# A scheduled attention loop: VectorE's scores issued every three tiles in a free row group, its value products and the transposes moved, the key tail in four small products

## The reference, cut to what matters

```python
def _L0_xattn_ref(query, key_value, Wq, bq, Wk, bk, Wv, bv, Wo, bo):
    ...
    q = (query @ Wq + bq).reshape(B, Nq, H, D).transpose(0, 2, 1, 3)
    k = (key_value @ Wk + bk).reshape(B, Nkv, H, D).transpose(0, 2, 1, 3)
    v = (key_value @ Wv + bv).reshape(B, Nkv, H, D).transpose(0, 2, 1, 3)
    attn = jnp.einsum('bhqd,bhkd->bhqk', q, k) * scale
    attn = jnp.clip(attn, -CLAMP, CLAMP)
    attn = jax.nn.softmax(attn, axis=-1)
    ...
    x = jnp.einsum('bhqk,bhkd->bqhd', attn, v).reshape(B, Nq, Cq)
    return x @ Wo + bo

x = x + _L0_xattn_ref(_layernorm(x, axis=-1), ctx_768, ...)
x = x + _L0_ffn_ref(_layernorm(x, axis=-1), ...)
```

## Time and profile before

| what | us |
|---|---|
| median of 3 runs | 830.57 |
| lowest, highest | 828.7, 833.89 |
| the profiled execution's own time | 830.38 |
| its span (first to last instruction) | 828.6 |
| TensorE busy with products | 748.6 |
| ScalarE busy | 726.7 |
| VectorE busy | 553.2 |
| exps of the loop (L497), 500 | 680.2 |

### The profile page before, as it was taken

The page is one execution under the profiler, slowest core; times in us unless marked ns, Lnnn a source line. Parts: engine busy times, 40 slices in busy tenths (PEclk is TensorE's granted clock), DMA queues, the critical chain, the costliest instruction groups (busy, mean ns, idle before and its releaser), DMA issues.

```text
span 828.6 us, 13067 instructions
## 1 busy us (share of the span) xinstructions
PE 748.6 (90%) x5338; PEld 228.1 (28%) x5338; DVE 553.2 (67%) x760; ACT 726.7 (88%) x587; POOL 20.7 (2%) x36
## 2 busy tenths in 40 slices
PE   5988999999989998999899999999999999998788
PEld 3642222222222222222232222222222222221447
DVE  4643488589856885788932985888768886891220
ACT  3769999999989997999979999999999999997341
POOL 8000000000000000000000000000000000000000
PEclk9989999999999999999999999999999999998899
DMA  5268141111111111111111111111111110000010
GB/s 182 105 182 266 48 142 49 33 33 48 33 32 33 49 32 33 49 32 48 33 32 32 32 45 36 33 44 37 33 48 32 48 34 1 1 1 1 4 51 26
DMA packets 21084, 42.15 MB, mean 51 GB/s; under 512 B 3079, under 2 KB 6525, under 8 KB 21021
## 3 DMA queue, kind: packets, MB, share of 16 engines
q1 hardware_dynamic: 19996, 40.49, 16.4%
q0 software_dynamic: 480, 0.66, 0.2%
q10 hardware_dynamic: 544, 0.12, 0.1%
HBM read 33.13 MB, written 8.13 MB: 50 GB/s over the span
## 4 chain that ended last, share of the span: by engine, by line
PE 43%; ACT 27%; issue 21%; DVE 7%; DMA 1%; SPq 1%; POOLq 0%; POOL 0%; ACTq 0%; DVEq 0%
ACT region_ctxT L497 26%; PE po L1089 21%; PE ps L1028 11%; PE ps L1164 2%; PE po L1183 1%; PE po L931 1%; PE ps L920 1%; DVE dres L773 1%; DVE dres L770 1%; DMA region_ctx<-in_ctx 1%; DVE region_kT L767 1%; DVE dres L765 1%; PE po L1028 1%; PE po L1077 1%; PE ps L908 1%
## 5 line engine op out<-in xcount | busy, mean ns | idle before, releaser
L497 ACT ACTIVATE region_ctxT<-ps 128x1536 f32<-128x1536 f32 x500 | 680.2, 1516 | 37.2 <-PE ps L1028 36.9
L1089 PE MATMUL po<-region_ctxT,v 128*9 128x512 f32 x2984 | 394.4, 601 | 1.2 <-ACT region_ctxT L497 1.2
L1028 PE MATMUL ps<-qst,region_k 32*128 32x512 f32 x1492 | 252.3, 495 | 46.8 <-ACT region_ctxT L497 45.8
L1028 PEld LDWEIGHTS ps<-qst,region_k 32*128 32x128 f32 x1492 | 97.7, 182 | 411.4 <-ACT region_ctxT L497 361.1
L737 DVE TENSOR_SCALAR region_kT<-po 128x512 f32<-128x512 f32 x108 | 74.5, 689 | 136.9 <-PE po L1028 136.7
L740 DVE SCALAR_TENSOR_TENSOR region_kT<-region_kT,po 128x512 f32<-128x512 f32 x108 | 73.4, 680 | 0.4
L1089 PEld LDWEIGHTS po<-region_ctxT,v 128*9 128x9 f32 x2984 | 44.4, 88 | 103.4 <-issue 95.8
L776 DVE SCALAR_TENSOR_TENSOR dres<-region_kT,dres 128x1024 f32<-128x1024 f32 x54 | 66.1, 1225 | 1.8
L773 DVE SCALAR_TENSOR_TENSOR dres<-region_kT,dres 128x1024 f32<-128x1024 f32 x54 | 65.8, 1218 | 0.3
L765 DVE SCALAR_TENSOR_TENSOR dres<-region_kT 128x1024 f32<-128x1024 f32 x54 | 65.7, 1217 | 0.0
L767 DVE SCALAR_TENSOR_TENSOR region_kT<-region_kT 128x1024 f32<-128x1024 f32 x54 | 65.7, 1217 | 0.0
(11 more groups left out here) (191 smaller groups left out, 297.2 us busy)
## 6 DMA issues: line engine op xcount, KB each, us to landing
region_k<-k_dram SPq DMA_DIRECT2D x80, 320.0 KB, 3.2
k_dram<-kparts SPq DMA_DIRECT2D x18, 320.0 KB, 4.3
qst<-q_dram SPq DMA_DIRECT2D x16, 128.0 KB
region_ctx<-in_ctx SPq DMA_DIRECT2D x2, 624.0 KB, 9.8
q_dram<-region_k SPq DMA_DIRECT2D x2, 512.0 KB, 2.7
k_dram<-kparts SPq DMA_DIRECT2D x2, 322.0 KB, 5.4
region_ctx<-in_ctx SPq DMA_DIRECT2D x1, 576.0 KB, 8.0
xres<-in_x SPq DMA_DIRECT2D x1, 512.0 KB, 4.4
```

The costliest lines, as they stand in the source:

```text
L497: act.activation(probs[:, t % NPR, :], ps[t % NSB][:, :], ACT.Exp, scale=ESCALE).then_inc(exp_ready, 1)
L1028: return mm(dst, kst[r, kt * P:(kt + 1) * P], qst[r, g, queries], start=True, stop=True)
L1089: last = mm(dst[QUAD * j:QUAD * j + V9, :], w, src, start=first, stop=last_one, skip_group_check=True)
```

## The change

`D_PLAN` gets new tiles, another choice of blocks, and a new field with the order in which the four heads' scores are computed. The number of steps on VectorE stays 27 and the number of tiles 500. In the new plan

- the D scores lie three tiles apart in general (14 to 15 tiles for a D step before, 12 now), and each is of the head that the three scores ahead of it don't have; pass 7 has no D step, passes 1, 3 and 5 have five each;
- the D values lie in tiles that complete no step, 10 to 15 tiles behind the last score;
- the first D step of pass 1 is block 29 with its first score at tile 43; before it was block 34 at tile 52.

`NORM_GAP` goes from 2 to 4, and `EPI_AT` is spread from 13 to 22 tiles. The pass ends are tiles 64, 124, 186, 246, 309, 369, 432, 499 (64, 127, 188, 250, 313, 376, 438, 499 before). The tail's value product, one of 128 rows by 128 columns with zeros outside the four heads' blocks, becomes four of 32 rows by 9 columns.

```diff
-NORM_GAP = 2
-EPI_AT = [2, 4, 8, 10, 11, 12, 13]
+NORM_GAP = 4
+EPI_AT = [2, 5, 10, 13, 16, 19, 22]
...
 D_PLAN = [
-    (0, 49, (22, 26, 30, 33), 46),
-    (0, 48, (37, 41, 44, 48), 61),
-    (1, 34, (52, 56, 60, 69), 81),
...
+    (0, 39, (19, 22, 25, 28), (2, 3, 0, 1), 40),
+    (0, 49, (31, 34, 37, 40), (2, 3, 0, 1), 52),
+    (1, 29, (43, 46, 49, 52), (2, 3, 0, 1), 67),
...
-                        d, j = divmod(i, GH)
-                        p, kt, _, _ = D_PLAN[d]
+                        d, k = divmod(i, GH)
+                        p, kt, _, heads, _ = D_PLAN[d]
+                        j = heads[k]
                         last = scores(po[1 - pv_bank(pass_at(t))][:, :], p, kt, j)
...
-                        last = mm(dst[:, :], vtail[:, PASSES[p][0], :], probs[:, tile % NPR, m * BANK:(m + 1) * BANK],
-                                  start=first, stop=last_one, skip_group_check=True)
+                        for j in range(GH):
+                            r = slice(QUAD * j, QUAD * (j + 1))
+                            last = mm(dst[QUAD * j:QUAD * j + V9, :], vtail[r, PASSES[p][0], QUAD * j:QUAD * j + V9],
+                                      probs[r, tile % NPR, m * BANK:(m + 1) * BANK],
+                                      start=first, stop=last_one, skip_group_check=True)
...
-                                src = dres[:, i % 2, j * BANK:(j + 1) * BANK]
+                                k = D_PLAN[i][3].index(j)
+                                src = dres[:, i % 2, k * BANK:(k + 1) * BANK]
```

More of the change, by code:

```diff
@@ L85 @@
 D_PLAN = [
-    (0, 49, (22, 26, 30, 33), 46),
-    (0, 48, (37, 41, 44, 48), 61),
-    (1, 34, (52, 56, 60, 69), 81),
[L89 to L112, removed]
[27 rows of a table added]
 ]
-DKT = [[kt for p, kt, _, _ in D_PLAN if p == q] for q in range(NP)]
+DKT = [[kt for p, kt, *_ in D_PLAN if p == q] for q in range(NP)]
 STEPS = [(p, kt) for p in range(NP) for kt in range(FULL + 1) if kt not in DKT[p]]
@@ L120 @@
 PASS_END = [max(STEP_TILE[n] for n, (p, _) in enumerate(STEPS) if p == q) for q in range(NP)]
-VALUES = sorted([(t, 0, n) for n, t in enumerate(STEP_TILE)] + [(v, 1, d) for d, (_, _, _, v) in enumerate(D_PLAN)])
+VALUES = sorted([(t, 0, n) for n, t in enumerate(STEP_TILE)] + [(v, 1, d) for d, (*_, v) in enumerate(D_PLAN)])
 VALUES_PASS = [STEPS[i][0] if kind == 0 else D_PLAN[i][0] for _, kind, i in VALUES]
@@ L126 @@
 VALUES_OF_D = {i: n for n, (_, kind, i) in enumerate(VALUES) if kind == 1}
-SPARE = sorted([(t, "score", GH * d + j) for d, (_, _, at, _) in enumerate(D_PLAN) for j, t in enumerate(at)]
+SPARE = sorted([(t, "score", GH * d + k) for d, (_, _, at, _, _) in enumerate(D_PLAN) for k, t in enumerate(at)]
                + [(PASS_END[p] + NORM_GAP, "tokens", p) for p in range(NP - 1)])
 SPARE_OF = {(kind, i): n for n, (_, kind, i) in enumerate(SPARE)}
-D_ROWS = [GH * d + j for d in range(len(D_PLAN)) for j in range(GH)]
 def values_through(t):
@@ L145, in spare_of_segment @@
 def spare_of_segment(p, s):
-    return max([SPARE_OF["score", GH * d + GH - 1] + 1 for d, (q, kt, _, _) in enumerate(D_PLAN)
+    return max([SPARE_OF["score", GH * d + GH - 1] + 1 for d, (q, kt, *_) in enumerate(D_PLAN)
                 if q == p and kt // SEG_T == s], default=0)
@@ L760, in pair_until @@
                             if half == 0:
-                                p, kt, _, _ = D_PLAN[d]
+                                p, kt = D_PLAN[d][0:2]
                                 heads = slice(GH * PASSES[p][0], GH * (PASSES[p][0] + 1))
```

## The result

The changed kernel takes 839.03 us (median of 4 runs, 837.44 to 839.96) against 830.41 us for the kernel before in the same comparison: ratio 1.0082, 95% interval 1.0054 to 1.011. The profiled run took 837.44 us, its span is 835.7. It is slower by 0.8%, clear of the noise, and inside the 1% that I called "same" (the interval reaches 1.1%).

What follows compares the result with a forecast made beforehand. ScalarE's exps, 1.331 us apart, were taken to bound the kernel, with 51.1 us of loop stalls. The terms sum to 58.3 us, 7.2 more, so 830.4 + 7.2 = 837.6 us, range 828 to 849 (forecast's own 832 to 844).

Steps and rivals of the forecast that it cites:

- start, tiles 0 to 18: Start of the loop: stalls of 2.8 us, expected unchanged.
- load wait at tile 43: Pass 1's first D score waits for keys landing at 123.0 us; TensorE stands 10.5 us, loss with low clock 11.2 us.
- dense runs: Stretches with D scores three tiles apart: VectorE needs 17.7 us a D step against 15.97 for twelve tiles; 24.3 us lost.
- transposes at 68, 128, 190, 250, 373: Four tiles behind five pass ends: VectorE finishes its pair before the sums, 1.7 us each, 8.5 us together.
- pass end at 313: Last D score only five tiles ahead: 3.7 us late, TensorE idle 3.8, plus 1.6 for likely low clock, 5.3 us.
- epilogue of the first half: Same seven jobs over 22 tiles in place of 13: 4.5 us in place of 5.3.
- tile 43 is the 38th exp of the run from 62.53: Step in the load wait: puts tile 43 at 62.53 + 37 x 1.343 = 112.2 us.
- where it would be 1.93 + 7 x 1.331: Step for the transposes: the exp comes at 12.9 us after the last D score's release, where it would be 11.2.
- The tails: Four last keys' products at pass ends: taken to run side by side in 0.98 us, against 1.13 for one full product.
- the rival at 854 us: The four tail products run one after another, 2.4 us more of TensorE at each of eight pass ends; chance 0.08.
- The head order: All 108 D scores in free row groups: 20 us of TensorE, no gain of its own booked.
- More low clock: Rival: VectorE's waits idle TensorE oftener, 2.5 us each, two to four times: 842 to 847 us; chance 0.14.

Runs made afterwards that it cites:

- e1_light: Changed kernel with one of VectorE's five 1024-column products a pair left out, so the D steps' exponential is no longer right: 813.37 us, ratio 0.9782.
- e2_queries_late: Changed kernel with eight of the twelve query loads moved behind the first six segment loads of pass 1: 834.52 us, ratio 1.0033.
- e3_tail_keys_late: Changed kernel with VectorE's copy of the four last keys moved behind its third D score: 839.18 us, ratio 1.0083.
- e8_sums_first: Changed kernel with VectorE copying the sums and dividing at a pass end before finishing its pending pair, where the next step leaves room: 842.97 us, ratio 1.0128.
- e6_tail_whole: Changed kernel with the product of the four last keys as one matmul over 128 rows again: 838.15 us, ratio 1.0089.
- e5_head_order: Changed kernel with the heads of every VectorE step in fixed order 0, 1, 2, 3, so 78 of 108 D scores share a row group: 839.7 us.
- e4_both: Changed kernel with eight query loads moved behind pass 1's first six segments and the last keys' copy behind the third D score: 831.52 us, ratio 1.0007.
- e7_gap_two: Changed kernel with NORM_GAP back from 4 to 2 and EPI_AT back to ending at 13: 865.53 us, ratio 1.0386.
- e10_plan14_loads: Changed kernel with D steps 14 tiles apart, pairs finished early, query loads and last keys' copies moved later: 885.84 us, ratio 1.0635.

## Why the prediction was right, and where its steps were not

The forecast was 837.6 us, 832 to 844; it came out at 839.03, the profiled run at 837.44. The stalls were put at 58.3 and are 58.8 us, but two steps failed behind that sum, and that it is so close is in part luck. The start (1.1 us less), the stall at tile 24 (4.8 more) and the load wait (4.1 less) belong together, as shown below. That the dense runs lost 2.3 less and the transposes 3.0 more is chance.

| term | forecast | measured |
|---|---|---|
| start, tiles 0 to 18 | 2.8 | 1.7 |
| tiles 18 to 43 | 0 | 4.8 |
| load wait at tile 43 | 11.2 | 7.1 |
| dense runs | 24.3 | 22.0 |
| transposes at 68, 128, 190, 250, 373 | 8.5 | 11.5 |
| pass end at 313 | 5.3 | 5.4 |
| epilogue of the first half | 4.5 | 4.5 |
| 436 and the rest | 1.7 | 1.8 |

*The dense runs, right.* "A run of N pairs loses 0.86 (N - 1) + 0.14 - 1.41": the stretches forecast at 4.8, 5.9, 4.8, 2.2, 4.8 and 1.3 us lost 4.15, 5.6, 4.1, 1.7, 4.7 and 1.6. e1_light shows the cause: with a D step under 16 us they lose 2.9 together. In tiles 85 to 120 the exps are 1.43 us apart on average, not 1.47, since the first delays are taken up by TensorE's room.

*The load, right in its landing, wrong in its price.* The keys came at 123.1 us as forecast, and e2_queries_late shows why they are late. The failed step is "tile 43 is the 38th exp of the run from 62.53", which takes the tiles ahead as undisturbed. The first D score had moved from tile 22 to 19, ahead of VectorE's copy of the last keys, and I costed nothing there. The two errors cancel for a reason, which e3_tail_keys_late shows: the load lands at its own time, whatever happens before.

*The transposes, about right in size, wrong in cause.* I booked 1.7 us each as VectorE being late with the sums; it is 2.0 to 2.6, and e8_sums_first shows that it falls at none of the five by more than 0.2 when the sums come earlier. The step that failed is "where it would be 1.93 + 7 x 1.331": TensorE has no tile with room there, so the 11.2 us that I compared with were out of its reach. The sign I had given, that TensorE waits for the copy of the sums at pass ends, is there only at tile 313: VectorE was the cause as forecast, but TensorE waits 1.98 us where I had 3.8.

*The tails, right.* The Trainium skill, TensorEngine Tiling (Array Packing), "Gotcha 1: PSUM Pressure", says that different row tiles cannot access the same PSUM bank at once. Here four row tiles, each with its own column group, wrote one bank in 0.97 us together, which is as fast as rows of one kind. The measurement decides: the rival at 854 us was not there, and e6_tail_whole is at 838.15.

*The head order* was booked at nothing by itself; e5_head_order agrees for this kernel.

*More low clock* (842 to 847 us): one stretch came that the forecast did not hold, at tile 24. Those at tiles 43 and 313 were in its terms.

## What to carry to other kernels

Where two engines hand work to each other through a single buffer, total work does not tell whether the one keeps up: play the jobs through in order, with the traces' durations, and look at how late each one is. With 27 D steps each, one table with its rule for finishing a pair took 886 us and another table with another rule 801; which of the two did it was not tried apart. Move the loads that nobody needs yet behind those that somebody waits for, and expect a gain ahead of a wait with a fixed end to be swallowed by it. When a change names what it improves, undo that part alone: here the head order and the four small tails were worth nothing that could be told, the distance of the transposes 26 us under this table, and the loss came from the table: VectorE's pace in the dense runs (e1_light) and the early first scores (e4_both).

## What the runs showed of the hardware

Four products of 32 rows in four row groups and four column groups, writing one PSUM bank, ran together: eight instructions in 0.97 us (kernel after), against 1.05 us for the same tail as two full instructions (e6_tail_whole).

An idle time of TensorE near 2 us can come with the lower clock, and does not always: 1.80 and 1.98 us (kernel after, 86.8 and 516.5 us), 2.13 us (e7_gap_two, 251.5 us) and 2.45 us (e10_plan14_loads, 185.1 us) came with it, the 2.35 us of the earlier trace rows did not. In e7_gap_two a wait of 2.13 us and the lower clock behind it cost 4.6 us of stall (6.9 at that pass end in place of 2.3).

A load of 320 KB issued at 109.7 us behind the twelve query loads took 13.3 us to land (kernel after), and one issued at 109.8 us 3.2 us with eight of them moved away (e2_queries_late).
